# Four mixture layers of a hybrid model: row buffers for every tile, bias tables cleared by ScalarE, biases split earlier

## The reference

```python
logits = x @ gate_w.T + gate_b
topk_logits, topk_idx = jax.lax.top_k(logits, K)
topk_weight = jax.nn.softmax(topk_logits, axis=-1)
# rows sorted by expert, then for every expert:
gate = jax.lax.ragged_dot(xt, w_gate, group_sizes) + b_gate[gid]
up = jax.lax.ragged_dot(xt, w_up, group_sizes) + b_up[gid]
gate = jnp.minimum(gate, 7.0); up = jnp.clip(up, -7.0, 7.0)
activated = (up + 1.0) * gate * jax.nn.sigmoid(1.702 * gate)
outs = jax.lax.ragged_dot(activated, w_down, group_sizes) + b_down[gid]
y = jnp.sum(outs * topk_weight[..., None], axis=1)
```

## Time and profile before

| | us |
|---|---|
| median of 3 runs | 4206.21 (4204.41 to 4208.45) |
| profiled execution, its own time | 4202.31 |
| its span, first to last instruction | 4200.6 |

### The profile page before, as it was taken

How to read it: one execution, slowest core, us unless ns; L and a number is a source line. 1 busy time by engine, 2 the same in 40 slices (tenths; PEclk the granted TensorE clock), 3 DMA queues, 4 the chain that set the end, 5 groups by cost and what they waited for, 6 DMA issues and landing times. The chain is left out here.

```text
span 4200.6 us, 68597 instructions
## 1 busy us (share of the span) xinstructions
PE 3276.3 (78%) x19706; PEld 2591.1 (62%) x19707; DVE 2831.2 (67%) x6281; ACT 2240.0 (53%) x5922; POOL 1801.6 (43%) x3107
## 2 busy tenths in 40 slices
PE   7799947916888379079999999999647399999274
PEld 3355545715776267058778878788545288888253
DVE  5699946746777566378768778588363388888542
ACT  3699802405777134068768678588212266665021
POOL 0399913567663145636446356356138200000265
PEclk9799967968999589589999999999757699999566
DMA  2011132430000335310000000000324300000524
GB/s 83 24 48 48 43 141 78 138 103 15 1 1 1 141 95 137 98 50 19 18 11 19 14 14 19 11 18 19 129 64 67 101 1 1 1 1 1 178 50 103
DMA packets 133310, 221.36 MB, mean 53 GB/s; under 512 B 28912, under 2 KB 106608, under 8 KB 131264
## 3 DMA queue, kind: packets, MB, share of 16 engines
q1 hardware_dynamic: 99216, 147.84, 10.6%
q0 software_dynamic: 33792, 69.83, 7.5%
HBM read 162.60 MB, written 54.80 MB: 52 GB/s over the span
## 5 line engine op out<-in xcount | busy, mean ns | idle before, releaser
L1256 POOL DMA_INDIRECT ex_xr<-scratch_rows,mo_token x288 | 286.6, 995 | 347.5 <-issue 312.0
L598 POOL TENSOR_TENSOR sc_h<-sc_h,sc_c 128x512 f32<-128x512 f32 x256 | 326.9, 1290 | 193.4 <-DVE sc_h L635 185.3
L3029 DVE TENSOR_TENSOR sa_pT<-bank,sa_pT 128x512 fp32r<-128x512 f32 x512 | 329.9, 686 | 34.2 <-ACT sa_pT L2897 30.3
L2889 ACT ACTIVATE sa_p<-bank,sa_nm 128x512 f32<-128x512 f32 x512 | 346.7, 689 | 2.5 <-DVE sa_nm L3020 2.5
L635 DVE TENSOR_TENSOR_SCAN sc_h<-sc_da,bank 128x512 f32<-128x512 f32 x256 | 311.1, 1220 | 37.9 <-ACT sc_da L578 22.9
L2718 PE MATMUL bank<-sa_kT,sa_qT 128*128 128x512 f32 x1024 | 333.4, 437 | 1.5 <-DVE residual L2996 1.5
L3016 DVE TENSOR_REDUCE sa_mx<-bank 128x2 f32<-128x1024 f32 x256 | 312.2, 1220 | 26.4 <-PE bank L2720 22.0
L1370 ACT ACTIVATE ex_xT<-bank 128x256 f32<-128x256 f32 (+1 forms) x288 | 105.1, 365 | 416.6 <-PE bank L1304 395.5
L2742 PE MATMUL bank<-sa_pT,sa_v 128*128 128x256 f32 x2048 | 301.4, 290 | 16.9 <-DVE sa_pT L3029 16.3
L1322 PE MATMUL bank<-mo_w_gu,ex_xT 128*128 (+2 forms) x1152 | 311.9, 399 | 1.3 <-issue 0.7
L2742 PEld LDWEIGHTS bank<-sa_pT,sa_v 128*128 128x128 f32 x2048 | 260.4, 190 | 39.3 <-DVE sa_pT L3029 28.7
(11 more groups left out here) (401 smaller groups left out, 9417.2 us busy)
## 6 DMA issues: line engine op xcount, KB each, us to landing
scratch_ys<-ex_yo SPq DMA_DIRECT2D x192, 128.0 KB
mo_w_gu<-in_w_gu SPq DMA_DIRECT2D x2, 9216.0 KB, 27.3
sc_c<-scratch_c SPq DMA_DIRECT2D x64, 256.0 KB, 3.2
sa_share<-scratch_shares SPq DMA_DIRECT2D x256, 64.0 KB, 2.6
mo_w_dn<-in_w_dn SPq DMA_DIRECT2D x2, 4608.0 KB, 48.0
mo_w_dn<-in_w_dn SPq DMA_DIRECT2D x2, 4096.0 KB, 33.3
scratch_rows<-ln_stage POOLq DMA_DIRECT2D x64, 128.0 KB, 5.5
ex_xr<-scratch_rows,mo_token POOLq DMA_INDIRECT x288
```

Of the source, the lines that this page charges most:

```text
L598: pool.tensor_tensor(h, h, C[u], ALU.mult).then_inc(used.sem, 1)
L1256: pool.indirect_dma_start(xr[u][:, :], None, rows, bass.IndirectOffsetOnAxis(ap=token[:, i:i + 1], axis=0), bounds_check=rows.shape[0] - 1 ...
L2889: act.activation(pr[h][:, :], SC[2 * s_ + h][:, :], ACT.Exp, bias=nm[:, col:col + 1], scale=SCALE, accum_out=rs[:, col:col + 1]).then_inc( ...
L3029: dve.tensor_tensor(spot(1), PT[h][:, :].rearrange("p (k n) -> p k n", k=TPB), spot(0).bitcast(F32), ALU.subtract).then_inc(*inc("kept_d"))
```

## The change

It has three parts. The ring of `ln_stage` has one buffer for each of the 16 tiles where rows are written, and the wait for the write of an earlier tile is gone; the four semaphores that count the writes stay. The two tables of biases are cleared by ScalarE, by copies of a zero tile, at the start of its program in the routing block, instead of by GpSimd memsets. The split of the biases moves from the end of VectorE's program in the routing block into `add_bias`, ahead of the wait for the logits; the three parts are allocated in an outer scope for this.

```diff
-        RING = 4 if rows is not None else 2
+        RING = TILES if rows is not None else 2
...
-                            .then_inc(rows[1][i % RING].sem, 16)
+                            .then_inc(rows[1][i % 4].sem, 16)
...
                     if i >= RING:
                         dve.wait_ge(turned.sem, turned.at(i - RING + 1))
-                        if rows is not None:
-                            dve.wait_ge(rows[1][i % RING].sem, rows[1][i % RING].at(16 * (i // RING)))
...
                 def add_bias(dve):
                     if which == 0:
                         dve.wait_ge(loaded.sem, loaded.at(16 * len(LOADS)))
+                        sp_ = Steps(dve, bsplit)
+                        sp_.then(dve.tensor_copy(bparts[0][:, :], braw[:, :]))
+                        sp_.then(dve.tensor_tensor(braw[:, :], braw[:, :], bparts[0][:, :], ALU.subtract))
+                        sp_.then(dve.tensor_copy(bparts[1][:, :], braw[:, :]))
+                        sp_.then(dve.tensor_tensor(braw[:, :], braw[:, :], bparts[1][:, :], ALU.subtract))
+                        sp_.then(dve.tensor_copy(bparts[2][:, :], braw[:, :]))
                     dve.wait_ge(logit.sem, logit.at(1))
...
-                        for b in (b_gu, b_dn):
-                            pool.memset(b[:, :].bitcast(F32), 0.0).then_inc(blanked.sem, 1)
...
                 @block.scalar
                 def _(act):
+                    if cap is None:
+                        for b in (b_gu, b_dn):
+                            dst = b[:, :].bitcast(F32).rearrange("p (r n) -> p r n", n=D_MODEL)
+                            act.activation(dst, c.zeros[:, :].bitcast(F32).rearrange("p (r n) -> p r n", r=1)
+                                           .to_broadcast([P, dst.shape[1], D_MODEL]), ACT.Copy).then_inc(blanked.sem, 1)
                     act.wait_ge(expd.sem, expd.at(1))
                     act.activation(wk, wk, ACT.Exp).then_inc(expd.sem, 1)
```

More of the change, by code:

```diff
@@ L783, in moe @@
             iota_e = sq("mo_iota_e", [P, max(NT, P)])
+            if which == 0:
+                bparts = [sq(f"mo_bpart{i}", [E, GU + D_MODEL], BF16) for i in range(3)]
             with ExitStack() as qq:
@@ L835, in moe @@
                 texp = sq("mo_texp", [NT, 1])
-                bparts = [sq(f"mo_bpart{i}", [E, GU + D_MODEL], BF16) for i in range(3)]
                 rowi, tilei = sq("mo_rowi", [P, TK], I32), sq("mo_tilei", [P, TK], I32)
@@ L1051, in _ @@
                                                  in1=blank[0:ROWS, :], op0=ALU.add, op1=ALU.add)
[L1052 to L1059, removed]
                     moe.own = st.n
```

## The result

The kernel after takes 4155.4 us (median of four runs, 4148.2 to 4156.7), beside 4206.1 for the kernel before: a ratio of 0.9876, 95% interval 0.9858 to 0.9893. It is faster by 51 us, where 4090 and a gain of 116 were forecast, and it lies outside the range of 4070 to 4125. Between the two profiled executions the gain is 54.1 (spans 4200.6 and 4146.5).

A forecast was written before the change was run, and what follows sets the result against it. VectorE's waits for row writes were taken to bound the norms. Norms 91.5, cast 9.2 and split 16.2, less 0.8 for the Exp, gave 116.1 us saved and 4090 us; own range 4080 to 4100, wider range 4070 to 4125.

The forecast's parts named there:

- The bound: Four norms: VectorE's waits for row writes set the end; with sixteen buffers TensorE sets the pace, saving 91.5 us.
- the cast: Routing block, first two mixtures: VectorE's cast no longer held until GpSimd's memset ends, saving 9.2 us in all.
- the split: First two mixtures, token table to first gather: bias steps and stores fall away, 8.1 us each, 16.2 in all.
- the Exp: Routing block, first two mixtures: ScalarE's Exp of the weights, queued behind the clears, loses 0.4 us each, together 0.8.
- the upper bound: Routing block, first two mixtures: with a 1.20 us gap after its table load, the Exp is 0.8 us late in each.
- the cover of the writes: Norm's end: GpSimd issues sixteen writes in 8.6 us, before TensorE finishes; the block's end does not wait for their landing.
- the first rival: Norms: GpSimd's queue takes only four writes, or the block's end waits for them; 22 us saved, about 4160; chance 0.11.
- a sign of being wrong: Norm: GpSimd's write issues stretch beyond 0.54 us or end after TensorE.
- The clock: Norms: TensorE's clock goes to 2.4 GHz, saving 3.7 us more in each of four mixtures, 4075; chance 0.08.
- No row write came too late for a reader: Rival, third and fourth mixtures: rows land too late for tags and gather, 67 us each, about 4283; chance 0.03.
- Part given back by code gaps: Rival, several places: late code fetches or the stages behind cost 10 to 40 us, 4100 to 4130; chance 0.08.

The follow-up runs named there:

- the kernel with kept buffers: Kernel after, with the 16 row buffers kept alive beyond the norm and the norm's block ended without GpSimd's drain: 4087.0 us, ratio 0.9715 to the kernel before.
- the control: Kernel after, with the row buffers kept alive beyond the norm and GpSimd's drain at the block's end kept: 4149.9 us, ratio 0.9868 to the kernel before.

## Why the prediction was wrong

**The bound was right.** VectorE's waits for the row writes held the norm, and with sixteen buffers TensorE sets its pace: without the drain the norms are shorter than before by 16.1, 16.0, 31.7 and 30.2 us, beside 16.2, 16.2, 28.5 and 30.6 forecast. (Of the third, 3.3 are gaps in the statistics loop, the ones of the earlier trace rows, which did not come back.) The terms for the cast (9.2), the split (16.2) and the Exp (0.8) sum to 24.6 beside 25.7 read from the trace. The 0.8 was not lost at all: the Exp ended 0.4 us before the sum needed it, and the gap that the upper bound rested on was a wait for VectorE, misread as part of a table load.

**The step that failed** is the cover of the writes: "they are now outstanding across the end of the block. Does that end wait for DMAs? ... So it did not, for SP's queue; for GpSimd's no row shows it". The argument from the earlier trace rows was correct for SP, as the rows issued by SP confirm, and I let it stand for GpSimd. There it fails: the end waited 66.5 us at four places, some 65 more than a block's end takes otherwise. 116.1 less 65 is 51, which is the measured gain. With that wait taken away, the kernel with kept buffers runs at 4087 us, against 4090 forecast. That the two are so near is in part luck: the 3.3 us of gaps count in the gain, and single executions of that kernel lie between 4080 and 4090.

**The rival named it.** "Or the block's end waits for GpSimd's writes" stood in the first rival, with 0.11 and about 4160. I had tied it to another mechanism, a queue that takes only four writes, and argued against that one alone; the sixteen issues without a gap show that the queue's depth was no limit. Some issues did stretch, to 0.98 us, which was named as a sign of being wrong; it cost nothing, since the sixteen were done nine us or more before the logits. The rival's price, 5.5 us for each norm, came out at 7.3 (29.2 over four), or 6.5 without the 3.3 us of gaps. A wait on landing deserved a chance of its own, since nothing in the rows spoke against it.

**The other rivals.** The clock did not rise. No row write came too late for a reader: SP's tags and the gather came behind a block that had already waited for the rows. Part given back by code gaps: not seen.

**What stays open.** Between the third norm's end and the fourth's start the kernel without the drain takes 819.9 us and the kernel after 816.0 (the kernel before: 818.3). VectorE's added wait for the rows is 1.0 us, in place of 0.5 for TensorE, so it accounts for some 0.6 of these 3.9 us; the rest has no cause shown. Why one landing takes 19 us in one norm and 35 in another was tied to the loads as a whole, not to one of them.

## What to carry to other kernels

A wait that is removed from a loop has to be looked for again at the next point where the engine that owns the transfer must be done: here the end of GpSimd's block waited for what the ring had waited for. Where transfers are to outlive a block, keep their buffers alive and end the block without that drain, or see that they land early by moving the bulk loads away from them; either is worth 63 to 66 us here beside the control on the same chip, and both together no more. When one of two clauses of a doubt is refuted, the other keeps its chance.

## What the runs showed that was not expected

- GpSimd's end of a block waited for its DMAs to land, to about 1 us beyond the last landing; with SP or ScalarE as issuer the next block began up to 8 us before the last landing.
- ScalarE's queue took nine writes of 128 KB and held the tenth issue for 9.8 and 22.1 us while the weights loaded; GpSimd's took all sixteen at 0.54 to 0.98 us each. ScalarE's copies stood behind the stalled issue.
- A 128 KB write landed in 2.2 us (median) without the weight loads and in up to 35 beside 9 to 12 MB of loads.
- With TensorE busy with transposes and small products in all of 15 us, its granted clock stayed at 0.50.
